# Expert steps of a graph and mixture-of-experts layer: the four mixed steps stand behind the 27 early ones, the filling rows behind the fourth load

## The reference

```python
h0 = layernorm(x)                                   # 6250 x 256
scores = h0 @ Wg + bg                               # 8 experts
_, idx = top_k(scores, 2)                           # two experts for each row, weight 1 each
mask = one_hot(idx, 8).sum(axis=-2)
h = gelu(einsum('td,edh->teh', h0, W1) + b1)        # hidden width 512
y = einsum('teh,ehd->ted', h, W2) + b2
out = x + einsum('ted,te->td', y, mask)
```

## Time and profile before

| | before |
|---|---|
| time, three runs | 2134.86, 2129.35, 2127.34 us; median 2129.35 |
| time of the profiled execution | 2129.58 us |
| its span | 2127.8 us |
| PE busy | 1876.3 us, 88% |
| PE weight loads | 1602.0 us, 75% |
| DVE / ACT / POOL busy | 1510.8 / 1192.1 / 1212.4 us |
| DMA | 422.38 MB |
| mean granted clock of PE | 0.943 |

### The profile page before, as it was taken

How to read it: one execution, slowest core, us unless ns; L and a number is a source line. 1 busy time by engine, 2 the same in 40 slices (tenths; PEclk the granted TensorE clock), 3 DMA queues, 4 the chain that set the end, 5 groups by cost and what they waited for, 6 DMA issues and landing times. The chain is left out here.

```text
span 2127.8 us, 43499 instructions
## 1 busy us (share of the span) xinstructions
PE 1876.3 (88%) x9692; PEld 1602.0 (75%) x9693; DVE 1510.8 (71%) x3661; ACT 1192.1 (56%) x2805; POOL 1212.4 (57%) x1207
## 2 busy tenths in 40 slices
PE   1995799999999999999999999878958699999994
PEld 1774688878778878777877777678847588878883
DVE  6885799999999999999999999985467611101110
ACT  2553577767677677677767776666456332223221
POOL 3336777777777777777777777200016754434443
PEclk9997999999999999999999999989955599999997
DMA  7767888888888878888888887177013666676673
GB/s 208 244 230 236 239 247 236 239 240 238 238 238 237 240 233 242 237 235 234 246 236 235 242 237 237 54 211 247 3 50 132 208 172 140 142 156 146 141 164 52
DMA packets 256715, 422.38 MB, mean 199 GB/s; under 512 B 45801, under 2 KB 128088, under 8 KB 256652
## 3 DMA queue, kind: packets, MB, share of 16 engines
q1 hardware_dynamic: 154608, 223.36, 33.7%
q0 software_dynamic: 65408, 153.31, 29.5%
q10 hardware_dynamic: 36636, 45.00, 6.7%
HBM read 358.65 MB, written 62.86 MB: 198 GB/s over the span
## 5 line engine op out<-in xcount | busy, mean ns | idle before, releaser
L830 POOL DMA_INDIRECT ring<-xl_rows,a_idx x928 | 889.0, 958 | 289.9 <-issue 252.9
L1147 PE MATMUL a_f_ps<-a_xr_w,a_hot_n 128*128 128x256 f32 x1856 | 528.9, 366 | 92.3 <-DMA ring<-xl_rows,a_idx 68.3
L1149 PE MATMUL a_f_ps<-ring,ident 128*128 128x256 f32 x1856 | 556.8, 381 | 0.0
L1147 PEld LDWEIGHTS a_f_ps<-a_xr_w,a_hot_n 128*128 128x128 f32 x1856 | 336.0, 191 | 213.3 <-issue 132.2
L1162 PE MATMUL a_o_ps<-ring,a_hot_e 128*128 128x264 f32 x1856 | 487.2, 387 | 2.4 <-DVE acc L1042 1.5
L1162 PEld LDWEIGHTS a_o_ps<-ring,a_hot_e 128*128 128x128 f32 x1856 | 347.1, 190 | 57.6 <-issue 3.7
L1005 DVE SCALAR_TENSOR_TENSOR a_pos<-a_f_ps,att_cols 128x512 f32<-128x512 f32 x464 | 314.5, 678 | 35.1 <-PE a_f_ps L1149 33.4
L1015 DVE TENSOR_REDUCE a_lg<-a_pos 128x8 f32<-128x512 f32 x464 | 315.0, 679 | 24.8 <-PE a_sm_ps L1172 24.1
L1029 DVE TENSOR_TENSOR ring<-ring,a_sm_ps (+1 forms) x464 | 314.2, 677 | 0.0
L1590 POOL DMA_INDIRECT out_dram<-ring,x_idx x106 | 165.9, 1565 | 233.9 <-issue 168.2
L911 ACT ACTIVATE a_hot_e<-a_far_e,one 128x512 f32<-128x512 f32 x232 | 167.6, 722 | 230.4 <-PE a_o_ps L1162 225.6
(11 more groups left out here) (383 smaller groups left out, 2584.2 us busy)
## 6 DMA issues: line engine op xcount, KB each, us to landing
a_xr_w<-xr_rows SPq DMA_DIRECT2D x464, 256.0 KB
a_rel_bc<-rel_rows ACTq DMA_DIRECT2D x116, 256.0 KB
ring<-in_L_ffn_W_dram SPq DMA_DIRECT2D x57, 512.0 KB, 4.2
ring<-xl_rows,a_idx POOLq DMA_INDIRECT x928, 3.5
xr_rows<-xr_parts SPq DMA_DIRECT2D x50, 256.0 KB, 2.1
ring<-disp_rows SPq DMA_DIRECT2D x49, 257.0 KB, 3.0
xl_rows<-xl_sb SPq DMA_DIRECT2D x50, 132.0 KB, 1.8
j_xl<-xl_rows SPq DMA_DIRECT2D x25, 264.0 KB, 2.9
```

The lines of the kernel that those rows point to most:

```text
L830: nc.gpsimd.indirect_dma_start(xl_e[:, p * T + 2 * h + u, :], None, k.xl_rows, bass.IndirectOffsetOnAxis(ap=idx[:, p, 2 * h + u:2 * h + u ...
L1147: nc.tensor.matmul(f_ps[:, slot(h), u, :], hot_n[:, j % 2, 2 * g + u, :], xr_w[:, h % XR, a, :].bitcast(F32R), start=(a == 0), stop=False)
L1149: last = nc.tensor.matmul(in_heads(f_ps[:, slot(h), u, :]), k.ident[:, :], heads_of(xl_e[:, p * T + 2 * h + u, :])[:, :, 0:C], start=False ...
```

## The change

Four things.

1. The steps that can be mixed are 27 to 30, right behind the early ones (`FIRST_MIXED = EARLY`, `PAST_MIXED = EARLY + MIXED`). Plain late steps 31 to 52 follow. As mixed steps use two w1 buffers each, four of them use eight, which is two rounds of the ring, so a plain step behind them finds w1 in the buffer of its own number again; the counts that PE waits for are 16 higher (`landings`). A w1 load of a plain step from 31 on waits for the step that used its buffer last: up(29) for steps 31 and 32, up(30) for 33 and 34, up(s-4) from 35 on.
2. In the table of late steps (`close`) the number of mixed steps is taken off all 26 late entries in place of the last four, so that full batches follow the mixed ones and empty steps, if there are any, come last.
3. `store_pads` stands behind the fourth load in place of the 27th. The three waits ahead of the late loads stay where they are.
4. PE does up(0) before it turns z of step 1.

```diff
--- before.py
+++ after.py
@@ -79,7 +79,7 @@
 EARLY_TILES = sum(GROUPS[:EARLY_GROUPS])
 EARLY = (K * P * EARLY_TILES - E * (BATCH - 1)) // BATCH
 LATE = SLOT_STEPS - EARLY
-FIRST_MIXED = SLOT_STEPS - MIXED
+FIRST_MIXED, PAST_MIXED = EARLY, EARLY + MIXED
 SPARE_FROM = E * D + 4 * 2 * (D + 1) + 2 * DH * BATCH + 2 * HC * BATCH + 4 * 2 * D + 4 * DH * HID
 ZW = D + 1
 
@@ -1531,10 +1531,13 @@
             return nc.values_load_multi_w_load_instructions(k.halves[:, 1, 2 * (s - FIRST_MIXED):2 * (s - FIRST_MIXED) + 2], engines=[engine], min_val=0,
                                                             max_val=E - 1)[1]
 
-        mixed = lambda s: isinstance(s, int) and s >= FIRST_MIXED
+        assert MIXED == RING
+        mixed = lambda s: isinstance(s, int) and FIRST_MIXED <= s < PAST_MIXED
 
         weight_of = lambda s, u: FIRST_MIXED + 2 * (s - FIRST_MIXED) + u
-        user_of = lambda n: n if n < FIRST_MIXED else FIRST_MIXED + (n - FIRST_MIXED) // 2
+        user_of = lambda n: n if n < FIRST_MIXED else FIRST_MIXED + (n - FIRST_MIXED) // 2 if n < PAST_MIXED + MIXED else n - MIXED
+        landings = lambda s, q, late: (s - q % RING) * (16 // RING) + (
+            32 if (s >= FIRST_MIXED if isinstance(s, int) else late) else 16)
 
         if True:
 
@@ -1559,7 +1562,10 @@
                     row = nc.values_load_multi_w_load_instructions(k.slots[:, 0, bass.ds(s, 1)], engines=[mybir.EngineType.SP],
                                                                    min_val=0, max_val=E * REGION)[1][0]
                     e = experts_of(mybir.EngineType.SP, s, 1)[0]
-                    wait_past(sp, up_done, 2 * (s - RING) + 2)
+                    if isinstance(s, int) and s >= PAST_MIXED:
+                        sp.wait_ge(up_done, 2 * user_of(s + MIXED - RING) + 2)
+                    else:
+                        wait_past(sp, up_done, 2 * (s - RING) + 2)
                     sp.dma_start(w1[:, q], k.We1[bass.ds(e, 1)].rearrange("o (h p) n -> p (o h) n", p=P)).then_inc(w1_in[q], 16)
                     wait_past(sp, y_ready, s - (RING - 1))
                     if isinstance(s, int) and s == 0:
@@ -1567,14 +1573,16 @@
                     sp.dma_start(z[:, q], k.disp_rows[bass.ds(row, BATCH), :].rearrange("(u p) w -> p u w", p=P)).then_inc(z_in[q], 16)
 
                 sp.wait_ge(k.table_ready, 1)
-                tiles(sp, EARLY, RING + EARLY % RING, RING, load)
+                for s in range(RING):
+                    load(s, s)
                 store_pads(sp)
+                tiles(sp, EARLY, EARLY % RING, RING, load, RING)
                 sp.wait_ge(k.table_ready, 2)
                 sp.wait_ge(k.late_scattered, 16 * K * (NT - EARLY_TILES))
                 sp.wait_ge(k.pads_stored, 16 * (E + 4))
-                tiles(sp, FIRST_MIXED, (FIRST_MIXED - EARLY) % RING, RING, load, EARLY)
-                for s in range(FIRST_MIXED, SLOT_STEPS):
+                for s in range(FIRST_MIXED, PAST_MIXED):
                     load(s, s % RING)
+                tiles(sp, SLOT_STEPS, RING, RING, load, PAST_MIXED)
 
             def additions(pool):
                 def store(s, q):
@@ -1591,14 +1599,15 @@
                                                      y[:, q, u], None, compute_op=ALU.add).then_inc(stored[q], 16)
 
                 tiles(pool, FIRST_MIXED, FIRST_MIXED % RING, RING, store)
-                for s in range(FIRST_MIXED, SLOT_STEPS):
+                for s in range(FIRST_MIXED, PAST_MIXED):
                     store(s, s % RING)
+                tiles(pool, SLOT_STEPS, (SLOT_STEPS - PAST_MIXED) % RING, RING, store, PAST_MIXED)
                 for q in range(RING):
                     pool.wait_ge(stored[q], 32 * len(range(q, SLOT_STEPS, RING)))
 
             def products(pe):
-                def turn_z(s, q):
-                    pe.wait_ge(z_in[q % RING], (s - q % RING) * (16 // RING) + (32 if mixed(s) else 16))
+                def turn_z(s, q, late=False):
+                    pe.wait_ge(z_in[q % RING], landings(s, q, late))
                     wait_past(pe, zt_ready, s - 1)
                     for h in range(DH):
                         for u in range(2):
@@ -1606,7 +1615,7 @@
                                                        z[:, q % RING, u, h * P:(h + 1) * P], k.ident[:, :])
                     last.then_inc(z_turned, 1)
 
-                def up(s, q):
+                def up(s, q, late=False):
                     pe.wait_ge(zt_ready, s + 1)
                     wait_past(pe, hid_ready, HC * s - HC)
                     if mixed(s):
@@ -1621,7 +1630,7 @@
                             if j % 2:
                                 last.then_inc(up_done, 1)
                         return
-                    pe.wait_ge(w1_in[q % RING], (s - q % RING) * (16 // RING) + 16)
+                    pe.wait_ge(w1_in[q % RING], landings(s, q, late))
                     for j in range(HC):
                         for h in range(DH):
                             last = nc.tensor.matmul(hid_ps[q % 2][:, j], w1[:, q % RING, h, j * P:(j + 1) * P], zt[:, q % 2, h],
@@ -1645,28 +1654,32 @@
                 nc.tensor.transpose(y_ps[0][:, 0, 0:E * HC], k.be1_rows[:, :],
                                     k.ident[0:E * HC, 0:E * HC]).then_inc(bias_turned, 1)
                 turn_z(0, 0)
-                turn_z(1, 1)
                 pe.wait_ge(k.experts_in, 16 * E)
                 up(0, 0)
+                turn_z(1, 1)
                 pe.wait_ge(bias_ready, 1)
 
-                def step(s, q):
+                def step(s, q, late=False):
                     e = experts_of_halves(mybir.EngineType.PE, s) if mixed(s) else experts_of(mybir.EngineType.PE, s, 1) * 2
-                    up(s + 1, q + 1)
-                    turn_z(s + 2, q + 2)
+                    up(s + 1, q + 1, late)
+                    turn_z(s + 2, q + 2, late)
                     down(s, q, e)
+
+                def late_step(s, q):
+                    step(s, q, True)
 
                 n = FIRST_MIXED - 2
                 pe.wait_ge(k.table_ready, 1)
-                tiles(pe, EARLY, EARLY % RING, RING, step)
+                tiles(pe, n, RING + n % RING, RING, step)
                 pe.wait_ge(k.table_ready, 2)
-                tiles(pe, n, (n - EARLY) % RING, RING, step, EARLY)
-                for s in range(n, SLOT_STEPS - 2):
+                for s in range(n, PAST_MIXED):
                     step(s, s % RING)
                 n = SLOT_STEPS - 2
+                tiles(pe, n, (n - PAST_MIXED) % RING, RING, late_step, PAST_MIXED)
+                e = experts_of(mybir.EngineType.PE, n, 2)
                 up(n + 1, n + 1)
-                for s in (n, n + 1):
-                    down(s, s, experts_of_halves(mybir.EngineType.PE, s))
+                down(n, n, e[0:1] * 2)
+                down(n + 1, n + 1, e[1:2] * 2)
 
             def units(act):
                 def take_zt(s, q):
@@ -1702,9 +1715,9 @@
                 act.wait_ge(k.table_ready, 1)
                 tiles(act, EARLY, EARLY % 2, 2, step)
                 act.wait_ge(k.table_ready, 2)
-                tiles(act, FIRST_MIXED, (FIRST_MIXED - EARLY) % 2, 2, step, EARLY)
-                for s in range(FIRST_MIXED, n):
+                for s in range(FIRST_MIXED, PAST_MIXED):
                     step(s, s % 2)
+                tiles(act, n, (n - PAST_MIXED) % 2, 2, step, PAST_MIXED)
                 for s in (n, n + 1):
                     gelu(s, s)
 
@@ -1725,8 +1738,9 @@
 
                 dve.wait_ge(k.bias_in, 16 * (E + 1))
                 tiles(dve, FIRST_MIXED, FIRST_MIXED % RING, RING, bias_down)
-                for s in range(FIRST_MIXED, SLOT_STEPS):
+                for s in range(FIRST_MIXED, PAST_MIXED):
                     bias_down(s, s % RING)
+                tiles(dve, SLOT_STEPS, (SLOT_STEPS - PAST_MIXED) % RING, RING, bias_down, PAST_MIXED)
 
         return loads, additions, products, units, biases
 
@@ -2164,9 +2178,7 @@
                     link(nc.vector.tensor_tensor_scan(odd_end[:, :], ones[0:1, 0:E], odd[:, :], 0.0, ALU.mult, ALU.add))
                     link(nc.vector.tensor_scalar(is_mixed[:, :], k.iota_row[0:1, 0:2 * MIXED:2], odd_end[:, E - 1:E], None, ALU.is_lt))
                     link(nc.vector.tensor_reduce(mixed_steps[:, :], is_mixed[:, :], AX.X, ALU.add))
-                    full = LATE - MIXED
-                    nc.vector.tensor_copy(slots[:, 0:full], k.iota_row[0:1, 0:full])
-                    link(nc.vector.tensor_scalar(slots[:, full:LATE], k.iota_row[0:1, full:LATE], mixed_steps[:, 0:1], None, ALU.subtract))
+                    link(nc.vector.tensor_scalar(slots[:, :], k.iota_row[0:1, 0:LATE], mixed_steps[:, 0:1], None, ALU.subtract))
 
                     rows, row, which_e = past[:, 0:LATE, :], slot_f[:, 0, 0:LATE], slot_f[:, 1, 0:LATE]
                     link(nc.vector.tensor_tensor(rows, slots[:, :, None].to_broadcast([1, LATE, E]), spread_s(end, LATE), ALU.is_ge))
```

(2 more changed lines are left out.)

## The result

| | before | after |
|---|---|---|
| median of the runs | 2129.31 us (4 runs, 2127.34 to 2134.86) | 2143.47 us (4 runs, 2138.74 to 2147.43) |
| profiled execution: span, own time | 2127.8, 2129.58 us | 2145.6, 2147.4 us |
| PE busy, mean granted clock | 88%, 0.94 | 88%, 0.94 |

The ratio is **1.0061, with a 95% interval of 1.0033 to 1.0089**: slower by 0.6%. The prediction was 2126.2 us with a range of 2115 to 2134. What came true is the rival to which it gave 0.09, the loads that fasten onto the stores, for which it had worked out 2140.5 us.

The account below looks back on a forecast made before the run. POOL's chain of store steps, not PE, was taken to set the end: 1927.5 us to step 27, 42 for mixed steps, 154.9 for plain ones, span 2124.4, 3.4 less than before; time 2126.2 us, range 2115 to 2134.

Parts of the forecast that it names:

- the loads that fasten onto the stores: Slower rival, chance 0.09: late y ties z and w1 to store landings; plain steps 8.3 us, time 2140.5 us.
- The mixed four: POOL's four mixed steps, moved among loads: 10.5 us each, 42 us in all, bounds 35.3 and 48.5.
- I take PE's own 7.35: Plain steps from 31 that run among loads, 15 of 22: 7.35 us each, 110.2 us.
- 5.8 to spare: Time in us by which a z load, landing in 3.8 us, beats its use 9.6 us after issue.
- the 154.9 of the sum: POOL's plain steps 31 to 52 to the end: 110.2 among loads, 38.6 for six quiet ones, 6.1 for the last.
- The threshold of 21.4: Lag in us of POOL's stores behind y from which y, awaiting its buffer, is late, and z behind it.
- a backlog forecast at 30 us: Lag of POOL's store behind its y at step 31: 17.6 us at step 27, plus 12.6 from the mixed steps.
- nothing on the path: Filling rows issued near 1702 to 1708 us on SP delay nothing that matters; PE's 7.0 us loss goes.
- First up product: up(0) ahead of the second turn: y of step 0 1 us earlier; 0 at the end, at most 1 gained.
- The gap of 4.64 us: Wait after a plain step's second store, put down to z issued 1.0 us after that store.
- The melting: Faster rival, chance 0.20: POOL's lag shrinks, 15 plain steps at 6.7 us take 100.5; time 2116.5 us.
- following rival: Faster rival, chance 0.05: POOL follows PE, its 12.8 us lag stands again at the end; time 2110.6 us.

Follow-up runs that it names:

- e5: The changed kernel unaltered, run again on another chip: 2136.56 us, ratio to before 1.0041.
- e6: The changed kernel with eight buffers for y and its row numbers in place of four: 2125.04 us, ratio to before 0.9986.
- e7: The changed kernel with w1 of step s+1 issued ahead of z of step s on SP from step 31 on: ratio to before 1.0023.
- e11: The changed kernel with eight y buffers and its filling rows behind the twelfth load: 2127.03 us, ratio to before 0.9986.
- e12: The kernel before with only the filling rows moved, behind the fourth load: 2127.99 us, ratio to before 0.9978.
- e8: The kernel before with POOL's first addition waiting until four y are ready: 2146.85 us, ratio to before 1.009.
- e9: The kernel before with POOL's first addition waiting until three y are ready: 2132.21 us, ratio to before 1.0009.
- e4: The changed kernel with its filling rows behind the twelfth load, on a slower chip: 2466.36 us, ratio to before 0.9981.
- e2: The changed kernel without the moved filling rows and with the old first product order, on a slower chip: 2474.2 us, ratio to before 1.0019.
- e3: The kernel before with only the filling rows moved, behind the twelfth load, on a slower chip: 2468.57 us, ratio to before 0.999.
- e10: e3 with the first up product ahead of the second turn: 2129.75 us, ratio to before 0.9995.

## Why the prediction was wrong

- **Frame: right.** POOL's chain sets the end, not PE. The mixed four: 42.6 us for 42. Step 27 is stored 206.5 us after POOL's first addition (1935.17 - 1728.71), where I had 201.9; in e5, e6, e7 and e11 it is 202.9, 203.5, 200.1 and 204.1. The mixed steps' loads cost what I gave them.
- **Start.** POOL's first addition is 3.1 us later in this profiled execution (1728.71). In e5 to e12, without e8 and e9 which delay it, it lies between 1723.87 and 1728.37, so I put this down to the spread of what lies ahead and not to the change.
- **The step that failed:** "I take PE's own 7.35, since the collision with the loads has held POOL to it wherever both ran on." The rows behind it were all of a backlog under 20 us, where PE is free and the collision adjusts itself to PE's pace. I had worked out myself that above 21.4 us y is late, but followed only z's use by PE from there ("5.8 to spare"), and not z's and w1's issue, which are what the store runs into. Above that backlog PE doesn't set the pace: POOL's landing, y, z and w1 close a ring without it, and PE follows 37 us later (2014.26). From step 31 to the end it took 2145.6 - 1977.78 = 167.8 us for the 154.9 of the sum, 12.9 of the 21.2 us between the forecast's span and 2145.6. The rest is 3.1 at the start, 4.5 to step 27 and 0.6 in the mixed steps.
- **The chance of that rival.** It was priced at 8.3 us a step and came out at 8.33 and 8.28. Two of its details did not: w1 came 0.2 to 0.7 us behind the second store in place of 1.2, and PE held by y was not what kept the pattern. The threshold of 21.4 is borne out from both sides: at 15.6 and 18.0 (e9, e4), and at 18.9 to 20.2 (e8, steps 26 to 43), POOL stays free; at 22.5 and 22.9 (e2 at step 33, e8 at its start) it is caught. e2's 21.2 at step 31 was still growing with every y on time. With a backlog forecast at 30 us, the threshold was passed by my own sum, and nothing spoke against the ring but the habit of the earlier trace rows. It deserved to be the forecast.
- **The Trainium skill's rule** ("DMA: Bandwidth & Descriptors", section "Queues, rings and completion order"), that each DMA engine takes turns between queues packet by packet, gave an estimate of at most 4.1 us for a gap. Fourteen gaps in a row at 4.5 to 5.2 don't agree with that estimate, and the measurement decides. It reckoned with one load beside the store and with turns of equal size; in these steps z is in flight as well, issued 1.5 to 1.6 us ahead of the second store. No run tests the rule itself.
- **Filling rows, "nothing on the path": half right.** PE lost 10 us at step 2 (7.1 in e5, 3.9 in e7, 1.3 in e6, nothing in e12), which I had not seen; why it varies so much is open. At the end it cost nothing: it only made POOL's backlog less (16.3 to 6.7 us), and POOL's way to step 27 was no longer with this loss (202.9 and 200.1 us in e5 and e7) than with nearly none (203.5 in e6).
- **First up product.** The time from y of step 0 to POOL's first addition grew from 13.0 to between 14.4 and 15.1 us in the kernels that have this edit; I had given 1 us of y, and nothing at the end. It was 1.4 to 2.1 us of y; nothing at the end is right as far as e3 and e10 show, which differ in this edit alone but ran on different chips (0.999 and 0.9995).
- **A reading that was too dear.** The gap of 4.64 us that I put down to z issued 1.0 us behind the second store is that of step 29 alone; in steps 27 and 28, with z at the same place, the gaps are 3.88 and 3.94. z is no bad place there, and e8 and e9 run free with it.
- **The melting and the following rival** would have needed store steps of 6.7. e4 shows such steps, 6.5 us, three in a row, from a backlog of 18 down: there is such a road, but it starts below the threshold.

## What to carry to other kernels

Where a slow consumer gives buffers back to the producer, work out the backlog at which the producer begins to wait, and treat it as a cliff: past it the producer's own loads are issued by the consumer's landings, at a fixed distance, and if that distance is a bad one it stays bad at every step until something long breaks it (in e8, by its rows, a wait of 10.54 us on PE). Before moving slow steps forward, count how many fast steps then run with the larger backlog; here four mixed steps at the end had nothing behind them, and in the middle they had fourteen. The cheap remedies are more buffers at that one place (e6: 11.5 us) or a start below the threshold. Turning the order of two loads that alternate in one queue is a weak one (e7: 4.3 us).

## What the runs showed of the hardware

- From the end of the issue of a step's second store (128 rows added onto the output) to the next store it takes 3.0 us with no load about. With loads it goes by the place of the 512 KB load. In plain steps 2 to 18 and 31 to 44 of all the traces here the median gap is 3.4 us with w1 issued 1.0 to 1.3 us ahead of the second store (24 steps; 3.2 in step 10 of after), 3.8 with 0.4 to 0.6 ahead (124 steps, nine in ten under 4.0), 4.8 with 0 to 0.7 behind (100 steps, 4.3 to 5.6). z moves along with w1, 0.7 to 3.3 us ahead of the store, so the two aren't told apart: with w1 0.1 to 0.3 ahead the median is 4.3 where z is more than 2 us ahead, and 4.5 in e7, where z is 1.5 ahead.
- Free running backlogs settle at a few values one PE step apart. On the mean they are 8.2 to 8.3 us (after, e5 and e7, steps 6 to 20), 15.4 to 15.6 (before's early steps, e6, e9, e10, e12) and 30.0 (e6, e11, steps 32 to 44), 7.35 apart or twice that. PE's losses of 10.0, 7.1 and 3.9 us at step 2 all led to the lowest of these (after, e5, e7), the loss of 1.3 to 15.6 (e6). Two more values, 12.1 (before and e9) and 19.4 (e8), stand behind the late filling rows, with z 1.0 us behind the second store. That they are stable is read from the rows; no run pushed one away from its value on purpose.
- With twelve filling stores, four steps' loads and POOL's scatters at once the DMA share went to 1.08, and a z load of 257 KB that lands in 3.8 us elsewhere took 16.7.
